# Cross attention: probabilities transposed by VectorE blocks and SBUF transfers instead of TensorE, with four projection banks and a new order of work

## The reference

```python
x = x + xattn(layernorm(x), ctx, ctx, mask, W_Q, W_K, W_V, W_O)   # ctx: 64 x 512 keys x 512
x = x + attn(layernorm(x), Wq, bq, Wk, bk, Wv, bv, Wo, bo)        # self attention, 64 tokens
x = x + ffn(layernorm(x), W1, b1, W2, b2)                         # ternary weights, 2048 hidden

def xattn(Q, K, V, mask, ...):
    q, k, v = split(Q @ W_Q.T), split(K @ W_K.T), split(V @ W_V.T)
    e = jnp.einsum('bhqd,bhkd->bhqk', q, k) / sqrt(32)
    e = jnp.where(mask, -jnp.inf, e)
    a = jnp.einsum('bhqk,bhkd->bhqd', softmax(e), v)
    return heads(a) @ W_O.T
```

## Time and profile before

| | |
|---|---|
| median of 3 runs | 1724.17 us (1723.85 to 1725.61) |
| the profiled execution | 1724.65 us, of which the span is 1722.8 us |
| mean granted TensorE clock | 0.992 |
| cross attention | up to about 751 us, steady from about 141 us on |
| handover to self attention | about 751 to 790 us |
| self attention | about 790 to 1255 us |
| feed-forward | about 1255 us to the end |

### The profile page before, as it was taken

How to read it: one execution, slowest core, us unless ns; L and a number is a source line. 1 busy time by engine, 2 the same in 40 slices (tenths; PEclk the granted TensorE clock), 3 DMA queues, 4 the chain that set the end, 5 groups by cost and what they waited for, 6 DMA issues and landing times.

```text
span 1722.8 us, 38414 instructions
## 1 busy us (share of the span) xinstructions
PE 1662.9 (97%) x16012; PEld 1390.8 (81%) x16012; DVE 1068.9 (62%) x1492; ACT 699.8 (41%) x1657; POOL 212.0 (12%) x300
## 2 busy tenths in 40 slices
PE   6899999999999999998999999999799999999999
PEld 4688888888878888876888888888688888888887
DVE  3655565555555565676688778787785455545633
ACT  2555556655556556665523222222222222222221
POOL 1000000000000000121202121211032022202200
PEclk9999999999999999999999999999899999999999
DMA  6011111111111111344111111111321122112110
GB/s 221 13 62 62 63 63 56 57 62 63 59 45 51 59 57 63 110 174 164 41 50 61 49 61 49 61 47 51 93 57 54 45 53 72 51 28 70 39 36 25
DMA packets 83484, 111.78 MB, mean 65 GB/s; under 512 B 7840, under 2 KB 48928, under 8 KB 82080
## 3 DMA queue, kind: packets, MB, share of 16 engines
q1 hardware_dynamic: 83360, 109.95, 20.2%
HBM read 67.97 MB, written 25.17 MB: 54 GB/s over the span
## 4 chain that ended last, share of the span: by engine, by line
PE 91%; DVE 5%; issue 1%; ACT 1%; DMA 1%; SPq 0%; DVEq 0%; ACTq 0%
PE project L350 51%; PE project L1285 13%; PE scores L718 4%; PE scores L1780 3%; PE scores L1778 3%; PE probs_t_psum L1780 3%; PE probs_t_psum L1778 3%; PE probs_t_psum L727 3%; PE attended_t L744 2%; PE probs_t_psum L1394 2%; PE attended_t L1413 1%; PE scores L522 1%; DVE self_at_lo L1597 1%; DVE self_residual L1633 1%; DVE row_sum L1622 0%
## 5 line engine op out<-in xcount | busy, mean ns | idle before, releaser
L1285 PE MATMUL project<-ff_xt,w_ternary 128*128 128x512 f32 x1024 | 253.1, 389 | 0.0
L1295 ACT ACTIVATE hidden<-project,b_sb 128x512 f32<-128x512 f32 x128 | 88.2, 689 | 339.0 <-PE project L1285 336.0
L1285 PEld LDWEIGHTS project<-ff_xt,w_ternary 128*128 128x128 f32 x1024 | 192.1, 188 | 39.8
L904 ACT ACTIVATE cross_scores_probs<-cross_scores_probs,exp_bias,logit_scale 128x128 f32<-128x128 f32 x256 | 122.8, 485 | 101.6 <-DVE exp_bias L1047 101.6
L350 PE MATMUL project<-self_xt_hi,self_w_hi 128*128 128x256 f32 x512 | 149.2, 291 | 2.7 <-DVE self_xt_lo L534 1.6
L350 PE MATMUL project<-self_xt_lo,self_w_hi 128*128 128x256 f32 x512 | 145.8, 285 | 0.0
L350 PE MATMUL project<-self_xt_hi,self_w_lo 128*128 128x256 f32 x512 | 145.7, 285 | 0.0
L904 ACT ACTIVATE cross_probs<-cross_scores,exp_bias,logit_scale 128x128 f32<-128x128 f32 x256 | 122.9, 485 | 1.8 <-DVE exp_bias L1047 1.8
L350 PE MATMUL project<-ctx_hi,cross_w_hi 128*128 128x512 f32 x256 | 106.1, 414 | 14.8 <-DVE ctx_lo L1066 14.8
L350 PE MATMUL project<-cross_w_hi,ctx_hi 128*128 128x512 f32 x256 | 108.7, 425 | 0.0
L350 PEld LDWEIGHTS project<-self_xt_hi,self_w_hi 128*128 128x128 f32 x512 | 99.2, 194 | 5.7 <-issue 2.6
(11 more groups left out here) (169 smaller groups left out, 4068.0 us busy)
## 6 DMA issues: line engine op xcount, KB each, us to landing
ctx_raw<-in_ctx SPq DMA_DIRECT2D x64, 256.0 KB, 3.8
cross_xt_raw<-in_x_t SPq DMA_DIRECT2D x64, 128.0 KB, 2.1
cross_x<-in_x SPq DMA_DIRECT2D x32, 256.0 KB, 2.9
x<-cross_x SPq DMA_DIRECT2D x32, 256.0 KB, 2.0
self_x<-x SPq DMA_DIRECT2D x32, 256.0 KB, 2.8
self_x_norm<-self_blocks_t SPq DMA_DIRECT2D x64, 128.0 KB, 2.7
ff_w_raw<-in_w SPq DMA_DIRECT2D x2, 4096.0 KB, 13.9
x<-self_residual SPq DMA_DIRECT2D x32, 256.0 KB, 2.0
```

Source lines behind the costliest of these rows:

```text
L904: last = nc.scalar.activation(c_p[buf][:, cols], c_s[buf][:, cols], ACT.Exp, bias=exp_bias[:, buf, g:g + 1], scale=logit_scale[:, parity(u ...
L1285: last = nc.tensor.matmul(PJ[m % 2][:], w1_q[:, c, cols], x_t[parity(v)][:, c].rearrange("p n a r -> p (n a r)"), start=(c == 0 and x_t is ...
L1295: nc.scalar.activation(h_raw[:, m % 2, :], PJ[m % 2][:], ACT.Relu, bias=b1_sb[:, m:m + 1]).then_inc(h_relu, 1)
```

## The change

What it does, in the cross attention of `LAST_TILE`:

1. TensorE's `transposes` and ScalarE's `probs_t_out` are gone. In their place VectorE does `probs_blocks` after each `divide`: one transpose of all 32x32 blocks from `c_p` into the scores buffer `c_s`. SP does `probs_gather`: four SBUF to SBUF transfers, each 32 partitions of 4 KB into 128 partitions of 1 KB, which complete the transposition in `c_pt`. The keys come interleaved: the copy out of the key projection (`keys_out`) and the mask bias read every fourth element, and `attend` reads its operand in two runs of 32. `c_pt` has two buffers. `maxima(q)` now also waits until the gather of batch q - 2 has read `c_s` (`pt_in`).
2. Four project banks instead of two: the PSUM tile of the transposes serves as banks 2 and 3.
3. A new order on every engine, below. TensorE's order in a unit was S0, O1 (previous), K0, S1, K1, T0, K2, A0, K3, S2, V0, T1, V1 with S3 in its middle, A1, V2, T2, O0, A2, Q0, T3, Q1, A3, V3, where S, T and A are scores, transposes and attend of a batch. It becomes S0, K0, S1, O1 (previous), K1, K2, S2, K3, A0, S3, V0, A1, V1, V2, O0, A2, Q0, Q1, A3, V3.
4. In the last unit self k0 moves ahead of scores 1; the first self queries Q0, Q1 and the self scores of tile 1 move ahead of the last output projection, which goes to another PSUM bank (`CROSS_LAST_O`); the first `self_maxima` moves into the cross stage.
5. `PE_FILLER`, 180 wait instructions of TensorE in the branch that is not run, becomes 0. Some SBUF tiles move.

```diff
+            def probs_gather(u, q):
+                wait(e, C.p_t, total(u, 4, q + 1))
+                wait(e, C.pv_done, total(u, 4, max(q - 1, 0)))
+                for a in range(4):
+                    e.dma_start(c_pt[q % 2][:, 256 * a:256 * a + 256],
+                                c_s[q % 2][32 * a:32 * a + 32, :]).then_inc(C.pt_in[q % 2], 16)
...
+                probs_gather(u, 0)
+                store_previous(u, kind)
+                probs_gather(u, 1)
+                if ahead:
+                    load_xt(later(u, 2))
...
+                probs_gather(u, 2)
+                probs_gather(u, 3)
+                if K.nt == 2:
+                    store(u, 0, kind)
...
-            def transposes(u, q):
-                wait(e, C.pt_ready, total(u, 4, q))
-                wait(e, C.p_norm, total(u, 4, q + 1))
-                for i in range(8):
-                    last = nc.tensor.transpose(PT[:, i * P:i * P + P],
-                                               c_p[q % 2][:, i * P:i * P + P], ident[:])
-                last.then_inc(C.pt_full, 1)
-
             def attend(u, q):
...
-                wait(e, C.pt_ready, total(u, 4, q + 1))
+                wait(e, C.pt_in[q % 2], total(u, 128, 64 * (q // 2 + 1)))
+                probs_t = c_pt[q % 2][:].rearrange("p (a i r) -> p a i r", a=4, r=32)
...
-                            c_pt[:, at:at + SEQ], start=(k == 0), stop=(k == K.kt - 1))
+                            probs_t[:, half:half + 2, tile, :],
+                            start=(k == 0), stop=(k == K.kt - 1))
...
-            def probs_t_out(u, q):
-                wait(e, C.pt_full, total(u, 4, q + 1))
-
-                wait(e, C.pv_done, total(u, 4, q))
-                nc.scalar.activation(c_pt[:], PT[:], ACT.Copy).then_inc(C.pt_ready, 1)
...
                 wait(e, C.s_full, total(u, 4, q + 1))
+
+                wait(e, C.pt_in[q % 2], total(u, 128, 64 * (q // 2)))
                 nc.vector.tensor_tensor(
                     rows(c_s[q % 2]), rows(S),
...
+            def probs_blocks(u, q):
+                wait(e, C.p_norm, total(u, 4, q + 1))
+                nc.vector.transpose(
+                    c_s[q % 2].rearrange("p (j i r) -> p i j r", j=4, r=32),
+                    c_p[q % 2].rearrange("p (i j k) -> p i j k", j=4, k=32)).then_inc(C.p_t, 1)
```

More of the change, by code:

```diff
@@ L76, with __init__ @@
 class Banks:
-    def __init__(self, prologue, full, last_but_one, last):
+    def __init__(self, prologue, full, last_but_one, last, banks=2):
         self.prologue = prologue
         self.uses = {"full": full, "last_but_one": last_but_one, "last": last}
-        self.first, self.per = len(prologue), len(full)
+        self.first, self.per, self.banks = len(prologue), len(full), banks
     def before(self, u, name=None, kind="full"):
@@ L95, in at @@
         j = self.before(u, name, kind)
[L96 to L104, removed]
+        bank, earlier = j % self.banks, j // self.banks
+        return bank, earlier if u is None else u.half * (2 * self.per // self.banks) + earlier
 def run_steps(eng, units, step):
@@ L602, in load_xt, with store, store_previous @@
                                 K.x_t[number(v), b]).then_inc(xt_in, 16)
+            def probs_gather(u, q):
[4 more added lines that the diff above has]
+                                c_s[q % 2][32 * a:32 * a + 32, :]).then_inc(C.pt_in[q % 2], 16)
+            def store(u, t, kind):
+                bank, before = K.banks.at(u, f"O{t}", kind)
+                wait(e, C.pj_free[bank], before + 1)
+                e.dma_start(K.x1[number(u), t], cx[parity(u)][0:K.tp, t, :]) \
+                    .then_inc(C.stored[parity(u)], 16)
+            def store_previous(u, kind):
+                if is_unit(u, 0):
+                    return
+                p = later(u, -1)
+                store(p, K.nt - 1, "last_but_one" if kind == "last" else "full")
+                if kind != "last":
+                    wait(e, C.stored[parity(p)], total_of_parity(p, 16 * K.nt, 16 * K.nt))
+                    load_x(later(u, 1))
             def step(u, kind):
-                more, ahead = kind != "last", kind == "full"
+                if kind == "last":
+                    last_step(u)
+                    return
+                ahead = kind == "full"
                 if ahead:
                     load_ctx(later(u, 2))
-                    load_xt(later(u, 2))
-                elif more:
+                else:
                     bank, before = K.banks.at(later(u, -1), "V3")
@@ L803, in step, with previous_output @@
                 scores(u, 0)
[L804 to L809 removed]
+                def previous_output():
+                    if is_unit(u, 0):
+                        e.wait_ge(w_lo_ready, 4)
+                    else:
+                        o_proj(later(u, -1), K.nt - 1, "last_but_one" if kind == "last" else "full")
                 if more:
```

280 lines of the change are left out of this document (144 added, 136 removed).

## The result

The changed kernel took 1706.03 us, median of 4 runs (1704.37 to 1707.19); the kernel before 1724.89, median of 4. The ratio is 0.9888, 95% interval 0.9873 to 0.9903. It is faster, by 18.9 us or 1.1%; forecast were 1669 us and a range up to 1687. The profiled execution took 1706.86 us, its span is 1705.1.

A forecast was written before the change was run, and what follows sets the result against it. TensorE was taken as the bound, busy 1662.9 of 1722.8 us. Saving 3.7 us in each of 14 unit intervals (52.0) plus 3.2 in the handover gives 55.2; 1724.65 less that is 1669 us, range 1657 to 1687.

The forecast's parts named there:

- What a group costs: TensorE, cross units: each group of 8 transposes costs 0.87 us; four leave each unit, 3.5 us.
- The floor of a unit: Steady cross unit, first scores to next first scores: 44.8 us falls to 41.1 if nothing is late, 3.7 saved.
- Is anybody late?: Layout of one cross unit: gathers land before their attends, no new TensorE wait; tightest is attend 2, 1.9 us to spare.
- The choice between two rows: Gather on SP, blocks to landing: 3.6 us by loads of transposed x, taken over 4.7 by the self stage's gather.
- The rival of a slow gather: Cross units: gather takes 4.7 us like self attention's, attend 2 waits 0.8 a unit, 11.6 in all: 1681; chance 0.13.
- its rule: Cross units: up to 4.4 us from blocks to landing nobody waits; above, about 2.6 us a unit per us.
- The rival of the gather as a bound: SP's transfers between block transposes and attends: gather of 7.0 us, units of 47.7, whole 1767; chance 0.04.
- The handover: First scores of unit 14 to first self transposes: 102.9 us to 99.7, gain 3.2, with waits of 15.4.
- one slow stretch less: Handover: of two 4 us stretches at the lower clock, losing 1.7 us each, one goes: 1.7 us gained.
- Code placement: Rival at TensorE's loop starts: seam doubling or appearing in other loops costs some 3 us each, 1675; vanishing, 1666; chance 0.08.
- Four banks: Projection banks in the cross units: four instead of two only loosen waits TensorE does not have; no gain counted.

The follow-up runs named there:

- the run without transposes: The kernel before without its 64 transpose groups and their copies in the cross stage, attend reading values in place of probabilities: 1707.53 us, units of 41.90 us.

## Why the prediction was wrong

**What a group costs** was right, if a little high: 0.87 forecast, 0.8 by the run without transposes. **The floor of a unit** was right: 41.1 forecast, 41.04 measured wherever gather 1 was on time.

**"Is anybody late?" failed, at batch 1.** The terms that were mis-sized all sit on SP, up to the landing of gather 1. The layout let SP be free for it 15.5 us into the unit; it was free at 17.4: gather 0 kept SP to 13.4 instead of 12.7, and the store, its landing and the reload held it 4.0 us instead of "some 3", with the store landing after 2.7 us, not 2.0. Then the gather itself took 5.0 instead of 3.6. Together 3.3 us, at a place where I counted 2.8 of room for attend 1 but had not followed what stood behind maxima 3: division 2, blocks 2 and gather 2, whose room was 1.9. I named the queue behind maxima 3 and did not carry the lateness through it. Where the prediction has no wait before the attends, the changed kernel waits at attends 1 and 2 in each unit and takes 43.1 us instead of 41.1; it takes 41.04 once gather 1 stands ahead of the wait for the store.

**The choice between two rows was wrong.** I took the loads' row since the pieces have the same number and size. The self gather's 2.62 and 2.7 were right: 2.5 and 2.6 to 2.9 measured. That source and destination both in SBUF is the trait that counts fits the issue, for the loads of transposed x still issue in 2.0 us beside the gathers; for the landing it is not shown, for there those loads take 2.5 us too, 3.0 with gather 1 in front, and 2.1 without gathers. The estimate of 2.3 us from the Trainium skill (DMA: Bandwidth & Descriptors, the anatomy of one DMA), whose fit is for transfers that GpSimd issues while SP issues these, is under the measured landing too; the measurement decides.

**The rival of a slow gather** had the right place, attend 2, and the right gather time, but a price of 0.8 us a unit; measured were 2.0, and the gather's own time is only 1.4 of the 3.3 us of lateness. And its rule, that time above 4.4 us is paid 2.6 times, does not hold: with gather 1 in front, 4.9 us cost nothing. What decides is when a gather can start. The rival of the gather as a bound did not come about. The Trainium skill's warning of strided copies (VectorE: DVE Perf Modes, the three transpose paths) does not bear on these gathers: landings of 2.6 to 2.9 us show no such slowness.

**The handover** was forecast 3.2 us shorter and came out 4.7 longer. Waits of 15.4 became 19.6: 1.8 of them are unit 14's gather waits, the self transposes waited 7.6 instead of 4.9, the first self keys 3.9 instead of 1.7. 2.8 of the 7.6 are VectorE's jump, which the prediction does not name. The clock fell further too, where I had counted on one slow stretch less, and TensorE's busy time is 88.0 us, 3.7 above the 84.3 of the sum. With the units repaired the handover is still 104.5, so this error stands by itself, some 5 us. The runs that moved work there only moved its waits; how to shorten it stays open.

**Code placement** was priced at 3 us a loop; it is worth 33. It did not decide here, because the change's filler fits its code. I also said that all of TensorE's code moves with the filler; only what lies behind the branch does. **Four banks** "only loosen waits that TensorE does not have" was true of the order before, and false of the new one.

## What to carry to other kernels

When a step moves to a queue, lay out the queue as carefully as the engine: a short transfer behind an instruction that waits for another's landing is as late as that landing, and one line of order was worth 31 us here. Between two rows for an unseen operation look first at the one with the same endpoints, expect transfers that are already there to land later beside the new ones (2.0 us became 2.7 here), and follow each lateness through everything that stands behind it. And where a kernel has loops of unrolled code, look at the start of each loop, and at the loading of its code, in every variant before reading its time: a difference there can be larger than the change.

## What was not expected

A run of 180 instructions that never execute is worth 33 to 34 us, by waits of up to 3.0 us at the start of the self loop and the lower clock behind them; in the run without transposes such waits reach 4.3 us. They come with the loop's code being loaded again in each pass. VectorE's jump over the unused branch takes 2.1 us or up to 6.5, by whether a 4 MB load is under way and its packet of code starts late.

The cross loop's waits of 0.6 us a pass, which the prediction put down to nothing that the profile shows, are of the same kind. From 240 to 640 us the kernel before loads 39 packets of code on q8, and each of the five waits ends 1.6 to 1.8 us after one of them; the changed kernel and the run without transposes, whose passes are 64 matmuls shorter, load none on that queue, and have no such wait.
